# Second attention layer: turns, projections and merges in one piece behind a chunk's value product, in place of between the scores

## The chip, the cores and the metric

One core of one Trainium2 chip runs the whole kernel in one launch. The metric is the device time in microseconds (us); the number shown for a kernel is the median of its runs. The kernel is a raw program: each engine (TensorE, VectorE, ScalarE, GpSimd, SyncE for transfers) has its own list of instructions, written out in order by the Python code, and the engines meet only at semaphores. An instruction that waits holds up everything behind it on its engine.

## The reference

Two decoder layers on x of 4 batches x 512 tokens x 128 features. The part that the change touches is the attention of the second layer (`A1`), 16 heads of 8 features, without a mask:

```
q = proj(wq, bq); k = proj(wk, bk); v = proj(wv, bv)      # 4 x 16 heads x 512 x 8
scores = einsum('bhqd,bhkd->bhqk', q, k) / sqrt(8)
attn   = softmax(scores, axis=-1)
ctx    = einsum('bhqk,bhkd->bhqd', attn, v)
out    = einsum('bsd,ed->bse', ctx, wo) + bo
x      = x + out
```

Before it come a causal attention (`A0`), a cross attention on 77 context tokens (`X0`) and a mixture of experts (`M0`); behind it a second cross attention (`X1`, one head of 128) and a quantized convolutional feed-forward (`F1`). Every layer starts with a layer norm of x.

## The kernel before

**Units and chunks.** Attention works in units of one batch and four heads. Units 0 to 15 are `A0`, 16 to 31 `X0`, 32 to 47 `A1` (four units a batch). A unit of `A1` has four chunks c = 0 to 3, one for each 128 keys. In a chunk TensorE makes four scores i = 0 to 3, one for each head (`scores_pe`, L712: 128 keys x 512 queries), ScalarE takes the exponential of each (`exp_act`, L733), and TensorE multiplies the values with all four (`pv_pe`, L760, eight instructions in the trace). The value product of chunk c is issued one chunk late, behind the fourth score of chunk c+1; that of chunk 3 stands in chunk 0 of the next unit (`last_pv_pe`).

**Maxima.** The softmax's maximum is found one to two units ahead: 16 products a unit (`max_pe`, L597, one head, 128 queries x 512 keys), each reduced by VectorE (`max_dve`, L613). `maxima_beside` puts four of them in each chunk, one ahead of each score. Score and maximum product use 64 rows of the array each, the one the upper and the other the lower half, and run side by side: below, such a two is called a pair. When a unit's 16 maxima are there, GpSimd splits them (`neg_of`, L628 and L630), TensorE turns them (`turn_pe`, L635), VectorE copies them (`turn_dve`, L642) and a transfer puts them beside the queries (`shift_sp`, L649); the first score of that unit waits for it.

**Banks.** `A1`'s scores rotate over three PSUM banks (`SINGLES = 3`): score n waits until the exponential of score n-3 is done (L708). Maxima, turns, merges, projections and the like take turns in four further banks (`take_bank`). `out` in `take_bank` says for how many later takes a bank is passed over; with `OPEN` it is passed over until `close_bank`.

**What stands between.** TensorE also carries work on all 128 rows. `finish_pe` (L779, four transposes) turns the finished unit's output, and VectorE normalises it (`finish_dve`, L788 and L792). `BESIDE` gives each unit at most one further task at each of the places "a", "b" and "c": `norm_pe` (task "turn", L546), `stage_q_pe` (q and k, L863), `stage_v_pe` (L881), `merge_pe` (L802), `proj_pe` (L821), and those of the second cross attention (`cross_*`). q, k, v and proj come in two halves (part 0 and 1); all others are whole in part 0. ScalarE or VectorE then empties the bank.

In `A1` before the change `unit_pe` (L1048 to L1096) places them so, behind the score of the number given:

- c = 0: "a" part 0 behind score 0; behind score 3 the last value product of the unit before, then "a" part 1
- c = 1: behind score 3 the value product, then "b" part 0
- c = 2: `finish_pe` behind score 0; behind score 3 the value product, then `turn_pe`
- c = 3: "c" part 0 behind score 0; behind score 3 the value product, then "c" part 1

In `A1`'s sixteen units there are 15 finishes, 10 whole tasks at "c", 6 whole tasks at "a", 6 at "b", and 9 in halves (6 at "a", 3 at "c"). ScalarE does the copy that empties a whole task's bank between a chunk's second and third exponential (`in_one` is true for them, L1154), that of a task in halves behind the fourth (L1165, L1171).

Of the kernel before, what the change touches and what calls it, by code (L numbers as in the profile page):

```python
# [128 lines left out]
STREAMS = (range(0, 2 * UN), range(2 * UN, 3 * UN))  # L129


def layer(g):
    return ATTS[g // UN]
# [53 lines left out]
def finished_in(g):  # L187

    u = g - (2 if layer(g) is X0 else 1)
    if g == X0.first:  # L190
        return None
    return u if u >= 0 and last_of_stream(u) == last_of_stream(g) else None
# [30 lines left out]

def in_one(g, place):

    return layer(g) is not X0 and BESIDE.get((g, place), ("q",))[0] not in ("q", "k", "v")


MOMENTS_IN = {5: (X0, 0), 9: (X0, 1), 13: (X0, 2), 19: (X0, 3), 23: (M0, 0), 27: (M0, 1), 31: (M0, 2), 32: (A1, 2), 33: (A1, 3), 37: (X1, 0), 40: (F1, 0), 41: (X1, 1),
# [32 lines left out]
def build(nc, d, out):  # L262
# [4 lines left out]
    with es:  # L267
# [364 lines left out]
        def turn_pe(e, g):  # L632
            e.wait_ge(s["neg"], g + 1)
            bank = take_bank(e, ("turn", g))
            e.transpose(bank[:].bitcast(BF16)[0:8 * QT, 0:P], neg[:, g % 2].rearrange("p j c h q -> p (j c h q)"),  # L635
                        identb[:]).then_inc(is_filled(("turn", g)), 1)
# [128 lines left out]
        def last_pv_pe(e, g):  # L765
            pv_pe(e, g, layer(g).kt - 1)
# [278 lines left out]

        def unit_pe(e, g):  # L1048
            a, u = layer(g), finished_in(g)
            first = g == STREAMS[0].start or g == STREAMS[1].start  # L1050
            short[0] = a is X0
            for c in range(a.kt):
                beside = maxima_beside(g, c)
                for i in range(4):
                    for k in beside[i]:
                        max_pe(e, *k)
                    scores_pe(e, g, c, i)
                    if a is X0:
                        continue
                    if i == 0:  # L1060
                        if c == 0:
                            beside_pe(e, g, "a", 0)
                        if c == 1 and a is not A1:
                            for t in turned_in(g):
                                turn_pe(e, t)
                        if c == 2 and u is not None:
                            finish_pe(e, u)
                        if c == 3:
                            beside_pe(e, g, "c", 0)
                    if i == 3:  # L1070
                        if c:
                            pv_pe(e, g, c - 1)
                        elif not first:
                            last_pv_pe(e, g - 1)
                    if i == 3:
                        if c == 2 and a is A1:
                            for t in turned_in(g):
                                turn_pe(e, t)
                        if c == 0:
                            beside_pe(e, g, "a", 1)  # L1080
                        if c == 1:
                            beside_pe(e, g, "b", 0)
                        if c == 3:
                            beside_pe(e, g, "c", 1)
                            if g == X0.first - 1:
                                turn_pe(e, X0.first + 1)
            if a is X0:
                for part in range(2):
                    beside_pe(e, g, "a", part)
                last_pv_pe(e, g - 1)  # L1090
                if u is not None:
                    finish_pe(e, u)
                if g + 2 <= last_of_stream(g):
                    turn_pe(e, g + 2)
                for part in range(2):
                    beside_pe(e, g, "b", part)  # L1096

        def unit_dve(e, g):
            a, u = layer(g), finished_in(g)
            for c in range(a.kt):  # L1100
                beside = maxima_beside(g, c)
                for i in range(4):
                    for k in beside[i]:
                        max_dve(e, *k)
                    if a is A1 and c == 2 and i == 3:
                        for t in turned_in(g):
                            turn_dve(e, t)
                    if a is not X0 and i == 0:
                        if c == 1 and a is not A1:
                            for t in turned_in(g):  # L1110
                                turn_dve(e, t)
                        if c == 2 and u is not None:
                            finish_dve(e, u)
                if a is not X0 and c != 2:
                    beside_dve(e, g, "abbc"[c])
                if c == 2 and a is A0 and g in NORM_IN:
                    after, b = NORM_IN[g]
                    normalise(e, after.ln, b)
                if c == 3 and g == X0.first - 1:
                    neg_of(e, X0.first + 1)  # L1120
                    turn_dve(e, X0.first + 1)
                if c == 2 and g in INTEGERS_IN:
                    scales_dve(e, INTEGERS_IN[g])
# [21 lines left out]
        def turned_in(g):  # L1145

            return [g + 1] if g < last_of_stream(g) else []
# [1375 lines left out]
```

## Time and profile before

| | us |
|---|---|
| median of 3 runs (lowest, highest) | 780.21 (778.45, 782.99) |
| the profiled execution | 780.1 |
| its span | 778.2 |
| TensorE matmuls busy | 642.7 (83%) |
| TensorE weight loads busy | 351.0 (45%) |
| VectorE busy | 561.7 (72%) |
| ScalarE busy | 431.2 (55%) |
| GpSimd busy | 302.7 (39%) |

The shares are means over six very different layers. `A1` lies at about 488 to 699 us of the span. Matmuls overlap in the pipeline, so a busy TensorE is not one at its peak; the distance from one start to the next says more than an instruction's own duration.

### The profile page before, as it was taken

How to read it: one execution, taken by the hardware profiler on the slowest of the kernel's cores; microseconds unless marked ns; L12 is line 12 of the kernel's file. 1: busy time of each engine (PE TensorE's matmuls, PEld its weight loads, DVE VectorE, ACT ScalarE, POOL GpSimd, SP SyncE). 2: the span in 40 equal slices, each digit the busy share in tenths (PEclk: the TensorE clock that was granted, in tenths of full speed). 3: DMA queues.
4: the chain of work that ended last, by engine and by line, in shares of the span. 5: the costliest groups of instructions: out<-in, count | busy, mean ns of one | idle time of the engine just before them, and what ended most of it. 6: DMA issues, size and time to landing. Idle time of an engine off the chain costs nothing.

```text
span 778.2 us, 16034 instructions
## 1 busy us (share of the span) xinstructions
PE 642.7 (83%) x5015; PEld 351.0 (45%) x5020; DVE 561.7 (72%) x1672; ACT 431.2 (55%) x825; POOL 302.7 (39%) x536
## 2 busy tenths in 40 slices
PE   5679998989888884099997695879999989897987
PEld 2344454445344443089997581213332323234543
DVE  6877688786657876657778346997898998924564
ACT  1415565655756551055554540658878777783644
POOL 6653444555533157613335633144330331422210
PEclk9967999999999997589999985789999999998999
DMA  7744563462233221211121254000421010000000
GB/s 228 258 173 140 170 205 113 131 196 79 75 105 93 82 76 44 71 36 49 51 82 58 66 166 145 29 28 29 159 87 56 29 55 30 1 1 1 14 14 28
DMA packets 72802, 67.17 MB, mean 86 GB/s; under 512 B 14560, under 2 KB 67232, under 8 KB 72720
## 3 DMA queue, kind: packets, MB, share of 16 engines
q1 hardware_dynamic: 69920, 61.21, 25.5%
q0 software_dynamic: 2272, 4.69, 1.9%
q8 instruction: 42, 0.69, 0.4%
q14 instruction: 40, 0.33, 0.1%
q10 hardware_dynamic: 528, 0.26, 0.1%
HBM read 37.74 MB, written 28.00 MB: 84 GB/s over the span
## 4 chain that ended last, share of the span: by engine, by line
PE 52%; DVE 23%; issue 10%; POOL 7%; ACT 4%; DMA 2%; SPq 1%; DVEq 0%; ACTq 0%; POOLq 0%
DVE mx L613 12%; PE bank_pv L760 11%; PE bank_turn L597 7%; PE bank_scores L2156 6%; PE bank_scores L712 4%; PE bank_turn L1888 4%; PE bank_scores L1896 3%; PE bank_scores L1888 3%; POOL routed_tokens L1849 2%; PE bank_turn L779 2%; DVE stats L468 2%; ACT probs L733 2%; PE bank_turn L601 1%; DVE xn L489 1%; PE bank_turn L821 1%
## 5 line engine op out<-in xcount | busy, mean ns | idle before, releaser
L613 DVE TENSOR_REDUCE mx<-bank_turn 128x1 f32<-128x512 f32 (+4 forms) x439 | 251.2, 611 | 47.8 <-PE bank_turn L601 29.0
L597 PE MATMUL bank_turn<-stk 64*128 64x77 bf16 (+4 forms) x695 | 150.4, 302 | 33.8 <-DVE mx L613 21.7
L712 PE MATMUL bank_scores<-stk 64*128 64x512 bf16 (+3 forms) x576 | 171.2, 359 | 4.6 <-ACT probs L733 3.4
L737 ACT ACTIVATE probs<-bank_scores 128x1024 f32<-128x1024 f32 (+4 forms) x160 | 116.8, 768 | 91.3 <-PE bank_scores L712 90.2
L733 ACT ACTIVATE probs<-bank_scores 128x512 f32<-128x512 f32 x256 | 139.3, 605 | 40.6 <-PE bank_scores L712 39.7
L760 PE MATMUL bank_pv<-probs,vsl 128*32 128x512 f32 (+3 forms) x1152 | 138.9, 555 | 2.9 <-POOL probs L745 1.8
L597 PEld LDWEIGHTS bank_turn<-stk 64*128 64x128 bf16 x695 | 51.4, 96 | 130.2 <-DVE mx L613 62.7
L745 POOL TENSOR_SCALAR_AFFINE_SELECT probs<-probs 128x256 f32<-128x256 f32 x128 | 51.5, 407 | 72.0 <-ACT probs L737 70.4
L1865 POOL DMA_INDIRECT expert_outputs<-probs,y_at x39 | 38.0, 975 | 94.8 <-DVE y_at L1762 58.4
L712 PEld LDWEIGHTS bank_scores<-stk 64*128 64x128 bf16 x576 | 45.5, 94 | 28.2 <-ACT probs L733 16.0
L495 POOL TENSOR_TENSOR rstd<-var,mhalf 128x4 f32<-128x4 f32 x24 | 24.7, 1029 | 85.4 <-DVE var L474 85.2
L613 DVE TENSOR_REDUCE mx<-bank_scores 128x1 f32<-128x512 f32 x72 | 49.0, 681 | 8.7 <-PE bank_scores L597 8.2
L601 PE MATMUL bank_turn<-masked_key,later_key 64*128 64x64 bf16 x512 | 51.1, 200 | 0.0
L601 PEld LDWEIGHTS bank_turn<-masked_key,later_key 64*128 64x128 bf16 x512 | 45.8, 102 | 11.3 <-issue 2.9
L2156 PE MATMUL bank_scores<-f_w1c,w 128*128 128x512 f32 x96 | 48.3, 643 | 0.4 <-ACT w L555 0.4
L1896 PE MATMUL bank_scores<-w,oT 128*128 x312 | 43.6, 285 | 2.5 <-DVE probs L1782 2.5
L1888 PE MATMUL bank_turn<-probs,w_now 128*128 128x128 f32 x320 | 43.4, 285 | 0.8 <-DVE probs L1761 0.8
L1888 PEld LDWEIGHTS bank_turn<-probs,w_now 128*128 128x128 f32 x320 | 41.3, 202 | 1.1 <-DVE probs L1761 1.0
L1896 PEld LDWEIGHTS bank_scores<-w,oT 128*128 128x128 f32 x312 | 39.6, 199 | 3.7 <-issue 3.5
L597 PE MATMUL bank_scores<-stk 64*128 64x512 bf16 x72 | 30.3, 421 | 11.7 <-DVE mx L613 11.4
L1888 PE MATMUL bank_scores<-probs,w_now 128*128 128x128 f32 x304 | 39.3, 275 | 0.1
L628 POOL CAST neg<-mx 128x16 bf16<-128x16 f32 x33 | 6.5, 196 | 82.6 <-DVE mx L613 81.9
(323 smaller groups left out, 1078.7 us busy)
## 6 DMA issues: line engine op xcount, KB each, us to landing
stk<-stack_A SPq DMA_DIRECT2D x64, 256.0 KB, 3.1
w<-in_M_w SPq DMA_DIRECT2D x12, 512.0 KB, 4.6
stack_A<-parts SPq DMA_DIRECT2D x12, 384.0 KB, 2.7
stack_A<-fill SPq DMA_DIRECT2D x8, 512.0 KB, 4.9
stk<-stack_X SPq DMA_DIRECT2D x16, 256.0 KB, 2.6
stack_A<-parts SPq DMA_DIRECT2D x12, 256.0 KB, 3.1
probs<-routed_tokens SPq DMA_DIRECT2D x39, 65.0 KB, 1.8
stack_A<-parts SPq DMA_DIRECT2D x12, 128.0 KB, 3.0
```

What stands on the lines that cost most here:

```text
L597: mm = e.matmul(o, stk[r, slot, 0, pp, qt * P:(qt + 1) * P], stk[r, slot, 1, pp, 0:keys], start=True, stop=not a.causal)
L601: mm = e.matmul(o[:, qt * P + HR * k:qt * P + HR * (k + 1)], later_keys(j, k), masked_keys(j), start=False, stop=k == 1)
L613: e.tensor_reduce(o.rearrange("p h q -> p q h"), bank_of((g, m))[:, 0:k * keys].rearrange("p (q h k) -> p q h k", q=len(tiles), h=len(hs)) ...
L712: mm = e.matmul(score_bank(g, kt, i)[:, 0:S - q0], stk[r, slot, 1, pp, kt * P:(kt + 1) * P], stk[r, slot, 0, pp, q0:S], start=True, stop=True)
L733: e.activation(probs[:, probs_of(g, kt), j + 2 * pp], score_bank(g, kt, i), ACT.Exp, scale=1 / math.sqrt(HD)).then_inc(s["probs"], 1)
L737: e.activation(probs[0:a.kp, probs_of(g, kt), j:HG:2, 0:n], bank_scores[0:a.kp, 2 * j:2 * j + 2, 0:n], ACT.Exp, scale=1 / math.sqrt(HD)).t ...
L745: e.affine_select(out=o, in_=o, compare_op=ALU.is_ge, fill=0.0, base=0, pattern=[[0, 2], [1, P]], channel_multiplier=-1).then_inc(s["maske ...
L760: mm = e.matmul(bank_pv[VW * h:VW * (h + 1), q0:S], vsl[:, slot, kt, h, :], probs[:, probs_of(g, kt), h, 0:S - q0], start=(kt == 0), stop= ...
L1865: e.indirect_dma_start(scr_y, bass.IndirectOffsetOnAxis(ap=y_at[:, t:t + 1], axis=0), y_sb[:, t % 2], None).then_inc(m["stored"][t % 2], 16)
L1888: mm = e.matmul(hid[t % 2][z][:, c * P:(c + 1) * P], w_now[:, t % 2, o:o + P], x_inT[:, t % 2], start=True, stop=True)
L1896: mm = e.matmul(y_bank[:, 0:D], act[:, t % 2, c * P:(c + 1) * P], w2[:, bass.ds(ex[t], 1), c, :].rearrange("p o n -> p (o n)"), start=(c = ...
L2156: e.matmul(bank, f_xT[:, b, j * P + tap:j * P + tap + P], f_w1c[:, tap], start=(tap == 0), stop=False)
```

## The change

All of it is in `A1`. Every full-row task is taken out from between the scores; `full_rows_pe` issues them behind the fourth score, in this order: the value product, in chunk 1 the finish, in chunks 0, 1 and 3 both halves of "a", "b" or "c", in chunk 2 the turn. The finish moves from chunk 2 to chunk 1, on VectorE too, where it now stands behind all four maxima of chunk 1. `in_one` is true for `A0` alone, so ScalarE empties the banks of all of `A1`'s tasks behind the fourth exponential. `maxima_beside`, the scores, the value products, GpSimd's and SyncE's lists stay as they are.

```diff
-    return layer(g) is not X0 and BESIDE.get((g, place), ("q",))[0] not in ("q", "k", "v")
+    return layer(g) is A0 and BESIDE.get((g, place), ("q",))[0] not in ("q", "k", "v")
...
+        def full_rows_pe(e, g, c):
+
+            if c:
+                pv_pe(e, g, c - 1)
+            elif g != STREAMS[1].start:
+                last_pv_pe(e, g - 1)
+            if c == 1 and finished_in(g) is not None:
+                finish_pe(e, finished_in(g))
+            if c != 2:
+                for part in range(2):
+                    beside_pe(e, g, "ab.c"[c], part)
+            if c == 2:
+                for t in turned_in(g):
+                    turn_pe(e, t)
+
         def unit_pe(e, g):
...
                     scores_pe(e, g, c, i)
                     if a is X0:
                         continue
+                    if a is A1:
+                        if i == 3:
+                            full_rows_pe(e, g, c)
+                        continue
                     if i == 0:
                         if c == 0:
                             beside_pe(e, g, "a", 0)
-                        if c == 1 and a is not A1:
+                        if c == 1:
                             for t in turned_in(g):
                                 turn_pe(e, t)
...
                     if i == 3:
-                        if c == 2 and a is A1:
-                            for t in turned_in(g):
-                                turn_pe(e, t)
                         if c == 0:
                             beside_pe(e, g, "a", 1)
...
-                    if a is not X0 and i == 0:
-                        if c == 1 and a is not A1:
+                    if a is A0 and i == 0:
+                        if c == 1:
                             for t in turned_in(g):
                                 turn_dve(e, t)
                         if c == 2 and u is not None:
                             finish_dve(e, u)
+                if a is A1 and c == 1 and u is not None:
+                    finish_dve(e, u)
```

## Rows read from the trace of the kernel before

**Rows 1.** Busy time by stretch of `A1`: from:to, length, then each engine.
```profile
526.00:564.00 38.00, 35.67 (x241) 11.73 (x239) 30.97 (x57) 30.56 (x57) 15.98 (x27) 0.99 0.29 95
564.00:635.00 71.00, 64.20 (x448) 21.59 (x444) 66.14 (x152) 56.22 (x109) 20.64 (x39) 1.00 0.18 55
635.00:681.00 46.00, 42.27 (x290) 14.06 (x289) 41.65 (x95) 36.01 (x72) 14.47 (x28) 1.00 0.08 25
```
**Rows 2.** TensorE in order of time, unit 38's chunks 1 and 2: start, length, instruction, [idle].
```profile
576.68 0.39 PE L712 MATMUL bank_scores<-stk 64*128 64x512 bf16 x1
...
577.95 0.39 PE L712 MATMUL bank_scores<-stk 64*128 64x512 bf16 x1 [0.24 <-ACT probs L733]
578.27 1.06 PE L760 MATMUL bank_pv<-probs,vsl 128*32 128x512 f32 x8
...
579.27 0.39 PE L712 MATMUL bank_scores<-stk 64*128 64x512 bf16 x1
579.59 0.66 PE L779 MATMUL bank_turn<-ident,oT 128*128 128x128 f32 x4
...
580.93 0.64 PE L760 MATMUL bank_pv<-probs,vsl 128*32 128x512 f32 x4
```
**Rows 3.** TensorE, unit 41's chunk 3 and the start of unit 42.
```profile
620.49 0.39 PE L712 MATMUL bank_scores<-stk 64*128 64x512 bf16 x1
...
621.97 1.06 PE L760 MATMUL bank_pv<-probs,vsl 128*32 128x512 f32 x8
...
623.25 0.39 PE L712 MATMUL bank_scores<-stk 64*128 64x512 bf16 x1
```
**Rows 4.** TensorE, a unit of `X0`: value product, finish, turn and projection in one piece.
```profile
229.00 1.06 PE L760 MATMUL bank_pv<-probs,vsl 128*32 128x512 f32 x8
229.99 0.66 PE L779 MATMUL bank_turn<-ident,oT 128*128 128x128 f32 x4
230.58 0.23 PE L635 MATMUL bank_turn<-identb,neg 128*32 128x128 bf16 x1
230.74 1.16 PE L821 MATMUL bank_turn<-A_wo,okT 128*128 128x128 f32 x8
231.83 0.21 PE L597 MATMUL bank_turn<-stk 64*128 64x77 bf16 x1
```
**Rows 5.** TensorE, units 34 and 35: k and v in halves.
```profile
531.81 0.39 PE L712 MATMUL bank_scores<-stk 64*128 64x512 bf16 x1
532.12 0.70 PE L863 MATMUL bank_turn<-xnT,A_wk 128*128 128x256 f32 x2
532.76 0.60 PE L712 MATMUL bank_scores<-stk 64*128 64x512 bf16 x2
...
533.67 1.07 PE L760 MATMUL bank_pv<-probs,vsl 128*32 128x512 f32 x8
...
537.43 0.39 PE L597 MATMUL bank_turn<-stk 64*128 64x512 bf16 x1 [0.56 <-DVE mx L613]
```
**Rows 6.** TensorE, unit 39's chunk 1: first and fourth score.
```profile
587.96 0.39 PE L712 MATMUL bank_scores<-stk 64*128 64x512 bf16 x1
...
589.85 0.39 PE L712 MATMUL bank_scores<-stk 64*128 64x512 bf16 x1 [0.59 <-ACT probs L733]
```
**Rows 7.** ScalarE in order of time, units 38 to 40.
```profile
579.79 0.60 ACT L733 ACTIVATE probs<-bank_scores 128x512 f32<-128x512 f32 x1 [0.42 <-PE bank_scores L712]
...
583.82 0.58 ACT L560 COPY xnT<-bank_scores 128x512 f32<-128x512 f32 x1
...
605.01 1.14 ACT L2080 ACTIVATE w<-bank_scores,x_rec 128x128 f32<-128x128 f32 x4 [1.11 <-PE bank_scores L2071]
```
**Rows 8.** VectorE in order of time, unit 38 (maxima and finish).
```profile
580.37 0.25 DVE L788 RECIPROCAL rec<-bank_turn 128x16 f32<-128x16 f32 x1
580.65 0.29 DVE L792 TENSOR_TENSOR otok<-bank_turn,rec 128x128 f32<-128x128 f32 x1
...
582.78 3.16 DVE L613 TENSOR_REDUCE mx<-bank_turn 128x1 f32<-128x512 f32 x5
```

## The prediction

> **What bounds the kernel now.** I read the shares by stretch first. In `A1` three engines are close together [rows 1]: between 526 and 564 us TensorE is busy 35.7 of 38 us and VectorE 31.0; between 564 and 635 VectorE leads with 66.1 of 71 (TensorE 64.2); between 635 and 681 it is 42.3 and 41.7 of 46. ScalarE is never above 81%. The granted clock is 0.99 to 1.00, the upper of the two levels, so distances can be added as they stand. A share so high does not say what a microsecond more on TensorE costs; for that I read the order of time chunk by chunk, from one value product to the next.
>
> The reader should look at two neighbouring chunks [rows 2]. In chunk 1 of unit 38 nothing stands between the scores: first score at 576.68, fourth at 577.95 after an idle stretch put down to the exponential (L733), value product at 578.27, which is 1.59 us behind the first score. Another bare chunk needs 1.48 (620.49 to 621.97) [rows 3]. Three banks hold the scores, so the fourth waits for the first exponential: it begins 0.4 to 0.5 us behind the first score's start (0.52 from 579.27 [rows 2] to 579.79 [rows 7]) and takes 0.60 [rows 7]. The pairs follow one another at 0.22, so TensorE would reach the fourth score at 0.66 and comes to it at 1.16: in each bare chunk a hole of 0.5 us. In chunk 2 the finish stands in that hole: first score 579.27, finish 579.59, value product 580.93, which is 1.66 us [rows 2]. The finish takes 0.59 until the next work starts (229.99 to 230.58) [rows 4] and lengthens the chunk by only 1.66 - 1.48 = 0.18 (by 0.07 against the other bare chunk). That is the observation on which the forecast rests: what stands between the scores is nearly free now.
>
> **What each kind of step costs behind the value product.** The first cross attention already has such a piece [rows 4]: product to finish 0.99, finish to turn 0.59, turn to projection 0.16, both halves of the projection to the next pair 1.09. From a value product straight to a pair it is 1.00 (578.27 to 579.27, the first maximum starting with its score) [rows 2]. So the piece adds each task's full length: 0.59 for four transposes, 1.09 for a projection.
>
> Gains first. Each entry from pairs into a full-row task costs 0.32 from the pair's start (579.27 to 579.59) [rows 2] where pair to pair costs 0.22 (the second L712 of the two in 0.60 that start at 532.76, each 0.38 long) [rows 5]: 0.10 a time. Taken out are 15 + 10 + 6 + 9 = 40 entries: 4.0 us. Halves joined cost 1.09 instead of twice 0.64 (532.12 to 532.76, the halves of q, k, v and the projection alike) [rows 4, 5], so 0.19 x 9 = 1.7 us. Together 5.7 us of TensorE work.
>
> The Trainium skill, "TensorEngine Tiling (Array Packing)", Key Properties, says that changing the tiling mode drains the engine; that rule speaks for the change. The trace agrees, with 0.10 us for an entry. By this rule alone the time falls by the 5.7 us above; it is the first rival below, since it is silent on who waits meanwhile.
>
> Now the cost, by chunk. A bare chunk is 1.48 + 1.00 = 2.48.
>
> *Finishes (15).* Chunk 2 with the finish inside is 1.66 + 1.00 = 2.66; with the finish ahead of it in chunk 1's piece it is 0.59 + 2.48 = 3.07: +0.41. Six units run so (34, 36, 37, 38, 41, 45): +2.4. In 35 a norm turn at "b" already precedes: I take +0.3. In 40 and 44 the four activations L2080, 1.14 us [rows 7], hold back the first exponential whether the finish is inside or not, so the finish comes on top: +0.5 each, 1.0. In 46 and 47 there are no maxima left, and a finish inside lengthens nothing: +0.5 each, 1.0. In 39 and 43 the finish chunk is already as slow as a bare one plus 0.59, since VectorE first has the cross scores: 0. In 33 and 42 VectorE sets the pace: 0. Sum 4.7.
>
> *Whole tasks at "c" (10).* Chunk 3 drops by the 0.18 that four transposes inside cost, and by up to 0.3 more where the copy between its exponentials held up the fourth score. The next chunk 0 gets 0.59 more, and ScalarE's copy (0.58 [rows 7]), until now between the second and third exponential, stands ahead of that chunk's first: four transposes last 0.66 and the next work starts after 0.59 [rows 4], so the copy runs until some 0.7 behind the next pair's start, the first exponential begins then instead of at 0.5, and the fourth score slips by 0.2. Net 0.59 + 0.2 - 0.4, +0.4 each in 36, 38, 43, 46, 47; nothing in 32, 33, 40, 42, 44, where VectorE's moments or scales stand next to them. Sum 2.0.
>
> *Whole tasks at "a" (6).* Moving them out makes chunk 0 bare and puts 0.59 to 1.09 behind it. Before, their ScalarE copy stood among chunk 0's exponentials, so that those and the copy of the last value product ran into chunk 1, whose fourth score came 1.89 us behind its first (587.96 to 589.85) in place of 1.16 [rows 6]. Behind the longer piece ScalarE has caught up but for the one copy. What is added to chunk 0's piece comes back in chunk 1. I take -0.3 over all.
>
> *Halves (9).* The half inside costs 533.67 - 531.81 = 1.86 against 1.48, so 0.38 [rows 5]; it goes, and the half behind (0.64) becomes 1.09: +0.07 each, 0.6 in all. Against that stands a bank: it is taken at the first half and kept open over three maxima, and the fourth maximum then waits for VectorE, 0.56 idle at 537.43 [rows 5]. Joined, the bank is out only for the piece. TensorE sits so about 2 us in all, but ScalarE's copies ahead of the next chunk give half of it back. Net about 0.6 - 1.0 = -0.4.
>
> *What VectorE takes back.* Its maxima follow one another at 0.60 to 0.63 (five in 3.16), four make 2.4 a chunk; a finish adds 0.5 [rows 8]. In its busiest stretch, 564 to 635, 4.9 of 71 us are not busy [rows 1]. Where it is the bound, a longer piece on TensorE costs nothing while its four banks hold work, 2.4 us, and the longest piece is about 1.00 + 0.59 + 1.09 = 2.68. I have set six chunks to nothing above; the rest of such cover I put at 1 us. The turned maxima are no new bound: where chunk 3 is bare, the next unit's first score comes 1.28 behind the value product (621.97 to 623.25) instead of 1.00 [rows 3], because it waits for the transfer; that is so now and stays so, and a task at "c" covers it in either order.
>
> Sum: 4.7 + 2.0 - 0.3 - 0.4 - 1.0 = +5.0 us. The gain of 5.7 is inside these distances and not to be taken off again. The profiled execution took 780.1 (span 778.2, 1.9 around it), 0.1 from the median: 780.1 + 5.0 = 785.1. The bounds of the cost: if every finish and "c" task cost its full 0.59 and every copy 0.3, 25 x 0.59 + 10 x 0.3 = 17.8, less what the chunks drop now (25 x 0.18 = 4.5) and less the bank stalls of 2: +11, 791. From below: the whole gain, -5.7, and the bank stalls, -2: 772.
>
> **Rivals.** *The switches decide (faster).* If the hole before the fourth score does not open, because ScalarE still has a backlog after each piece or the maxima fill it, TensorE's own work counts and 40 entries and nine joins come off: -5.7, 774.4. It decides where TensorE is the only bound. For it: 35.7 of 38 us busy at 526 to 564 [rows 1]. Against: ScalarE has no backlog even now (0.42 idle until the score at 579.79) [rows 7]; a longer piece makes it idle more, not less.
>
> *VectorE hides it (no change).* If VectorE is the bound through 564 to 681 (107.8 of 117 us [rows 1]), only the terms outside count: units 34 to 36 (+1.3) and 46, 47 (+1.8), less freed bank stalls of 1 to 2: 781.5. Against: 9.2 us of that stretch VectorE is not busy, and a wait that the piece adds ahead of its finish is new idle time on the very engine that should be the bound.
>
> *Starved by the piece (slower still).* In chunk 1 VectorE's finish stands behind four maxima and waits for a finish that TensorE issues behind the value product, and in 39, 40, 43 and 44 for a further task. If VectorE then starts late and its lag spreads to the next chunk's banks, 0.3 us more in 15 units: +4.5 on top, 789.6.
>
> **How the numbers follow.** The forecast's mechanism gets 0.50, with 782 to 788 as its own range; the switches 0.20; VectorE 0.22; starved 0.08. What can be told from no change is 0.5%, 3.9 us: 776.3 to 784.1. Of the forecast's 0.50 a fifth lies below 784.1; starved is all slower: 0.48. Faster: most of the first rival, 0.18. The same: the remaining 0.34. The range, 775.5 to 789.5, leaves some 0.1 on each side.
>
> **What would show it.** Right: in the trace after, almost every chunk of `A1` has three pairs at 0.22, then 0.4 to 0.6 us without a start, then the fourth score; ScalarE's idle time before L733 grows by several us; chunk 2 of 37, 38, 41 takes 3.0 to 3.1 from value product to value product; waits of maxima for VectorE at L597 shrink. Everything outside `A1` keeps its length within 1 us. Wrong: fourth scores that follow at 0.22 behind the third, or chunks with a finish ahead that still take under 2.8. Then the switches count and the time falls. If VectorE is without idle time from 564 to 681, the second rival is right. If TensorE's granted clock falls below 1.00 in the new holes, none of the sums holds.

## The result, and the profile after

| | before | after |
|---|---|---|
| median us (runs) | 780.33 (16) | 784.68 (16) |
| lowest, highest | 778.45, 784.82 | 780.48, 787.34 |
| ratio, 95% interval | | 1.0046 (1.0027 to 1.0065) |
| span of the profiled execution | 778.2 | 785.1 |
| first score of unit 32 to the last value product of unit 47 ("the layer") | 210.55 | 215.32 |

The change costs about 3.6 us (0.0046 x 780; by the interval 2.1 to 5.1); the forecast was 5.0 and a time of 785.1. The layer itself grew by 4.77 us in the profiled execution. From the page after, its groups of maxima and exponentials (instructions | busy, mean ns | idle before, and what ended most of it):

```profile
L597 PE MATMUL bank_turn<-stk 64*128 64x77 bf16 (+4 forms) x699 | 149.7, 303 | 32.3 <-DVE mx L613 23.2
...
L733 ACT ACTIVATE probs<-bank_scores 128x512 f32<-128x512 f32 x256 | 133.3, 605 | 37.1 <-PE bank_scores L712 36.7
```

The stretches that answer to [rows 1] lie 4 to 5 us later, and the middle one is 1 us longer (from:to, length, then busy time of TensorE, its weight loads, VectorE, ScalarE and GpSimd, then the granted clock):

```profile
530.00:568.00 38.00, 35.25 (x230) 12.61 (x230) 29.74 (x55) 28.88 (x56) 16.31 (x27) 0.99 0.27 89
568.00:640.00 72.00, 66.09 (x450) 22.02 (x449) 65.58 (x148) 54.87 (x108) 19.82 (x36) 1.00 0.18 57
640.00:686.00 46.00, 41.42 (x283) 14.20 (x283) 41.49 (x96) 35.78 (x72) 12.97 (x27) 1.00 0.08 25
```

VectorE and ScalarE are busy for a smaller share than before in all three: in the middle one VectorE is idle 6.4 of 72 us, where 4.9 of 71 were idle. The granted clock is as it was. What was lost was lost to waits, and where they stand is read chunk by chunk. Unit 38's chunks 1 and 2, the place of [rows 2], on TensorE (start, length, instruction; the maxima of the pairs are left out):

```profile
584.09 1.06 PE L760 MATMUL bank_pv<-probs,vsl 128*32 128x512 f32 x8
585.09 0.66 PE L779 MATMUL bank_turn<-ident,oT 128*128 128x128 f32 x4
...
585.68 0.39 PE L712 MATMUL bank_scores<-stk 64*128 64x512 bf16 x1
...
585.90 0.59 PE L712 MATMUL bank_scores<-stk 64*128 64x512 bf16 x2
...
586.84 0.39 PE L712 MATMUL bank_scores<-stk 64*128 64x512 bf16 x1
587.16 1.07 PE L760 MATMUL bank_pv<-probs,vsl 128*32 128x512 f32 x8
```

The finish is in front now, the three pairs follow at once, and from the third to the fourth score the hole of the forecast is open again. From unit 34's chunk 2 on, 42 of 54 chunks look like this (two scores at 0.22 to 0.3 us and the fourth over 0.55 behind the third); before the change it was 6. From value product to value product this chunk takes 3.07 us, where 2.66 stood [rows 2]: the forecast's number for it.

Not all of it is in this pattern. At the start of unit 41 stands a wait that the forecast had expected to shrink:

```profile
617.33 0.66 PE L802 MATMUL bank_scores<-ident,otok 128*128 128x128 f32 x4
617.92 0.39 PE L597 MATMUL bank_turn<-stk 64*128 64x512 bf16 x1
...
619.82 0.39 PE L597 MATMUL bank_turn<-stk 64*128 64x512 bf16 x1 [1.08 <-DVE mx L613]
...
620.14 1.06 PE L760 MATMUL bank_pv<-probs,vsl 128*32 128x512 f32 x8
```

VectorE at the same time computes the moments of the next layer norm between two maxima:

```profile
617.68 0.29 DVE L468 BATCH_NORM_STATS2 stats<-x_sb 128x6 f32<-128x128 f32 x1
...
619.00 0.17 DVE L474 TENSOR_SCALAR var<-mv 128x4 f32<-128x4 f32 x1
619.08 2.48 DVE L613 TENSOR_REDUCE mx<-bank_turn 128x1 f32<-128x512 f32 x4
```

The fourth maximum needs a bank. The merge (L802) has taken one of the four, and that one is passed over for the next four takes (`out=4`), which are exactly this chunk's four maxima. So the fourth needs a bank that one of the first three has used, and VectorE, on its moments from 617.68, gives it back too late.

### The profile page after: what moved, and what is told of

It is laid out like the page before. It is cut to its first block, busy times and chain, and to the rows that moved or that the text cites. A ratio compares the mean times of both kernels' runs of the same rounds, so it can differ in the third digit from the quotient of the medians.

```text
span 785.1 us, 16034 instructions
## 1 busy us (share of the span) xinstructions
PE 648.6 (83%) x5015; PEld 354.1 (45%) x5020; DVE 562.6 (72%) x1672; ACT 428.6 (55%) x825; POOL 302.7 (39%) x536
## 4 chain that ended last, share of the span: by engine, by line
PE 53%; DVE 24%; issue 9%; POOL 7%; ACT 3%; DMA 2%; SPq 1%; DVEq 0%; ACTq 0%; POOLq 0%
DVE mx L613 14%; PE bank_pv L760 12%; PE bank_turn L597 6%; PE bank_scores L2174 5%; PE bank_scores L712 4%; PE bank_turn L1906 4%; PE bank_scores L1914 3%; PE bank_scores L1906 3%; PE bank_turn L779 3%; POOL routed_tokens L1867 2%; DVE stats L468 2%; PE bank_turn L601 1%; PE bank_scores L597 1%; DVE xn L489 1%; PE bank_turn L863 1%
## 5 line engine op out<-in xcount | busy, mean ns | idle before, releaser
L613 DVE TENSOR_REDUCE mx<-bank_turn 128x1 f32<-128x512 f32 (+4 forms) x443 | 253.3, 613 | 46.4 <-PE bank_turn L601 29.6
L597 PE MATMUL bank_turn<-stk 64*128 64x77 bf16 (+4 forms) x699 | 149.7, 303 | 32.3 <-DVE mx L613 23.2
L712 PE MATMUL bank_scores<-stk 64*128 64x512 bf16 (+3 forms) x576 | 168.5, 360 | 6.8 <-ACT probs L733 4.8
L733 ACT ACTIVATE probs<-bank_scores 128x512 f32<-128x512 f32 x256 | 133.3, 605 | 37.1 <-PE bank_scores L712 36.7
L760 PE MATMUL bank_pv<-probs,vsl 128*32 128x512 f32 (+3 forms) x1152 | 140.6, 561 | 2.8 <-POOL probs L745 1.8
L597 PEld LDWEIGHTS bank_turn<-stk 64*128 64x128 bf16 x699 | 51.6, 97 | 123.6 <-DVE mx L613 57.2
L613 DVE TENSOR_REDUCE mx<-bank_scores 128x1 f32<-128x512 f32 x68 | 46.3, 681 | 8.6 <-PE bank_scores L597 8.2
L2174 PE MATMUL bank_scores<-f_w1c,w 128*128 128x512 f32 x96 | 46.1, 618 | 0.4 <-ACT w L555 0.4
L597 PE MATMUL bank_scores<-stk 64*128 64x512 bf16 x68 | 28.5, 418 | 13.2 <-DVE mx L613 13.1
```

Source lines behind the costliest of these rows:

```text
L597: mm = e.matmul(o, stk[r, slot, 0, pp, qt * P:(qt + 1) * P], stk[r, slot, 1, pp, 0:keys], start=True, stop=not a.causal)
L613: e.tensor_reduce(o.rearrange("p h q -> p q h"), bank_of((g, m))[:, 0:k * keys].rearrange("p (q h k) -> p q h k", q=len(tiles), h=len(hs)) ...
L712: mm = e.matmul(score_bank(g, kt, i)[:, 0:S - q0], stk[r, slot, 1, pp, kt * P:(kt + 1) * P], stk[r, slot, 0, pp, q0:S], start=True, stop=True)
L733: e.activation(probs[:, probs_of(g, kt), j + 2 * pp], score_bank(g, kt, i), ACT.Exp, scale=1 / math.sqrt(HD)).then_inc(s["probs"], 1)
L760: mm = e.matmul(bank_pv[VW * h:VW * (h + 1), q0:S], vsl[:, slot, kt, h, :], probs[:, probs_of(g, kt), h, 0:S - q0], start=(kt == 0), stop= ...
L2174: e.matmul(bank, f_xT[:, b, j * P + tap:j * P + tap + P], f_w1c[:, tap], start=(tap == 0), stop=False)
```

## The experiments

For each kernel I take from its trace the layer's length and that of a quieter stretch, from unit 34's chunk 2 to the layer's end. From there on (in time: from the start of the value product in that chunk) equal chunks of different kernels agree to 0.01 us, and the granted clock is 1.00 in all of them. The part ahead of it contains transfers and less regular waits, and its granted clock differs from one profiled execution to the next, from 0.77 to 0.83 where whole tiles are worked on. So a layer's length contains some chance of the clock, and the stretch does not. Ratios are against the kernel before in the same group of runs, with their 95% interval; the median of the kernel before was 779.7 to 782.8 in these groups.

| kernel | layer | stretch | ratio |
|---|---|---|---|
| before | 210.55 | 167.83 | |
| changed | 215.32 | 171.36 | 1.0046 (1.0027 to 1.0065) |
| finish_behind | 213.88 | 169.89 | 1.0051 (1.0021 to 1.0081) |
| whole_behind | 212.17 | 169.26 | 1.0008 (0.9980 to 1.0035) |
| halves_joined | 207.98 | 166.73 | 0.9997 (0.9972 to 1.0023) |
| behind_third | 207.55 | 166.34 | 0.9981 (0.9952 to 1.0009) |
| banks_back | 212.06 | 169.78 | 0.9983 (0.9950 to 1.0015) |
| third_joined | 206.23 | 165.52 | 0.9914 (0.9881 to 0.9947) |
| third_joined_back | 204.64 | 164.75 | 0.9932 (0.9904 to 0.9960) |
| copies_later | 215.21 | 169.34 | 1.0047 (1.0019 to 1.0074) |
| joined_later | 215.37 | 173.20 | 1.0070 (1.0037 to 1.0102) |
| short_between | 182.45 | 148.39 | 0.9639 (0.9597 to 0.9680) |
| short_behind | 188.69 | 150.81 | 0.9656 (0.9611 to 0.9701) |

A layer's length is of one profiled execution; the ratio is of all runs and decides on the whole. Its intervals are 1.5 to 3.5 us to each side.

### The finishes alone

```diff
-                        if c == 2 and u is not None:
+                        if c == 2 and a is A0 and u is not None:
                             finish_pe(e, u)
...                                       # i == 3, behind pv_pe
+                        if c == 1 and a is A1 and u is not None:
+                            finish_pe(e, u)
```

(VectorE's finish moves with it, as in the change.)

> The kernel before with the 15 finishes alone moved behind the value product of chunk 1, on TensorE and VectorE as the change has it. All other tasks stay between the scores. Theory (the hole before the fourth score is left empty): A1, from the first score of unit 32 to the last value product, grows from 210.6 us by the 4.7 of the forecast's finish term; chunk 2 goes from 2.66 to 3.07 us where no maximum waits. Rival (the switches decide): 15 entries at 0.10 go away, A1 shrinks by 1.5. Rival (VectorE hides it): under +1.5.

The layer grows by 3.33 us, the stretch by 2.06, and the kernel is slower, 1.0051. In the order of time (unit 37's chunk 2) the finish again stands ahead, and the fourth score comes late:

```profile
569.28 1.06 PE L760 MATMUL bank_pv<-probs,vsl 128*32 128x512 f32 x8
570.28 0.66 PE L779 MATMUL bank_scores<-ident,oT 128*128 128x128 f32 x4
...
572.04 0.39 PE L712 MATMUL bank_scores<-stk 64*128 64x512 bf16 x1
572.35 1.06 PE L760 MATMUL bank_pv<-probs,vsl 128*32 128x512 f32 x8
```

3.07 again. This part alone accounts for most of the loss, 2.1 of 3.5 us in the stretch. Of the 1.3 us ahead of it, 0.7 are not the finishes' at all. Unit 32's chunk 2 has the same instructions in both kernels, before and then here:

```profile
495.42 1.45 PE L760 MATMUL bank_pv<-probs,vsl 128*32 128x512 f32 x8
...
498.28 1.07 PE L760 MATMUL bank_pv<-probs,vsl 128*32 128x512 f32 x8
```

```profile
497.37 1.93 PE L760 MATMUL bank_pv<-probs,vsl 128*32 128x512 f32 x8
...
500.94 1.07 PE L760 MATMUL bank_pv<-probs,vsl 128*32 128x512 f32 x8
```

It takes 2.86 us at a granted clock of 0.86 in the one and 3.57 at 0.58 in the other.

### The whole tasks alone

```diff
+        def joined(g, place):
+            task = BESIDE.get((g, place), (None,))[0]
+            return layer(g) is A1 and task not in ("q", "k", "v", "proj")
...
-                        if c == 0:
+                        if c == 0 and not joined(g, "a"):
...                                       # "c" likewise; at i == 3, behind the product:
+                            if joined(g, "a"):
+                                beside_pe(e, g, "a", 0)
```

(`in_one` is true in `A0` alone, as in the change.)

> The kernel before with only the whole tasks at a and c (turns, merges, the cross attention's) moved behind the value product, and ScalarE's copies behind the fourth exponential. Finishes and the halves stay. Theory: +2.0 for the tasks at c and -0.3 for those at a, A1 +1.7 us. Switches decide: 16 entries, -1.6. VectorE hides it: within 0.7 of nothing.

The layer grows by 1.62 us, 1.43 of them in the stretch; over all runs 1.0008, which cannot be told from no change. The forecast's 1.7 is met, but not term by term. A task at "a" of 39, 43 and 47 makes chunk 1 longer by 0.51, 0.51 and 0.33, and this does not come back. Against that, chunk 3 of 42 alone falls by 1.46 (3.98 to 2.52), of which the next chunk takes 0.73.

### The halves alone

The same edit with `task in ("q", "k", "v", "proj")` and `in_one` as before.

> The kernel before with only the nine tasks in halves (q, k, v, projection) joined behind the value product. Theory: A1 -0.4 us (the bank is out for a shorter time, one half is no longer covered). Switches decide: nine entries and nine joins, -2.6. If the bank kept open over three maxima is what costs most: -2 or more as well, but then the waits of the maxima for VectorE in these chunks are gone, where the switches alone would leave them.

The layer shrinks by 2.57 us, where -0.4 was forecast; the whole time cannot be told from no change (0.9997). Where the forecast had looked, in 35 and 36, it was right: chunk 0 falls by 0.36 and chunk 1 grows by 0.44. The gain lies elsewhere. Unit 34's chunks 0 and 1 are together 1.2 shorter, and at the starts of units 41 and 45 the kernel before has the projection's first half between the scores and keeps its bank open, so that the fourth maximum waits for VectorE's moments:

```profile
610.71 0.39 PE L712 MATMUL bank_scores<-stk 64*128 64x512 bf16 x1
611.03 0.71 PE L821 MATMUL bank_turn<-A_wo,okT 128*128 128x128 f32 x4
...
613.33 0.39 PE L597 MATMUL bank_scores<-stk 64*128 64x512 bf16 x1 [1.05 <-DVE mx L613]
```

With the halves joined the chunk has all four banks:

```profile
607.39 1.06 PE L760 MATMUL bank_pv<-probs,vsl 128*32 128x512 f32 x8
608.39 0.39 PE L712 MATMUL bank_scores<-stk 64*128 64x512 bf16 x1
...
609.31 0.39 PE L597 MATMUL bank_turn<-stk 64*128 64x512 bf16 x1
609.79 0.39 PE L712 MATMUL bank_scores<-stk 64*128 64x512 bf16 x1
610.11 1.06 PE L760 MATMUL bank_pv<-probs,vsl 128*32 128x512 f32 x8
```

It takes 2.72 in place of 3.94 us (unit 45's 2.61 for 3.84). Two thirds of that come back within the unit: the whole projection stands ahead of chunk 1 (+0.48), and in chunk 2 VectorE is late instead (+0.33). What is left is 0.4 a unit.

### Into the hole, in place of out of it

If the hole before the fourth score is what makes an inserted task cheap, the best place is right ahead of that score, behind the third.

```diff
-                    if i == 0:
+                    if i == (2 if a is A1 else 0):
```

(On TensorE; the same on VectorE for the finish.)

> The kernel before with the inserted tasks behind the third score in place of behind the first, so right in the hole before the fourth; nothing is joined. Theory: the fourth score comes no later than now, and the second and third exponential and maximum come 0.6 us earlier, so ScalarE and VectorE wait less: A1 -2 us, between -5 and 0. If the place between the scores does not matter, only being among them: 0. If a task that sits in the hole delays the fourth score (task issued at 0.66, its end at 1.35, as now): also 0, with the same chunk of 2.66 us around a finish.

The layer shrinks by 3.00 us; over all runs 0.9981, whose interval holds 1. The chunk with the finish did not get shorter (2.73 against 2.67); half of the gain lies ahead of the stretch, and in the stretch, 1.5 us shorter, the largest gains are in chunk 1 of units 39 and 43, 2.79 in place of 3.20, and of 47, 2.80 in place of 3.38, and at the start of 41 and 45, 0.3 each. In 39's chunk 0, where the task stands, the second score now starts 0.23 behind the first in place of 1.38, and so its exponential comes earlier; in chunk 1 the first exponential then starts 0.78 behind its score in place of 1.19. The hole was well filled before; what it gains is that ScalarE is fed sooner.

### The parts together, and the banks

The three parts add up to 3.33 + 1.62 - 2.57 = +2.4, the change to +4.8. Set side by side chunk by chunk, the other 2.4 us stand in a few places: +1.0 at the start of unit 41 and +0.9 at that of 45 (less 0.3 in each one's chunk 2), +0.8 in unit 34 and +1.0 in 33's chunk 2, less 0.5 in 32's chunk 2, where the part with the finishes had the lower clock. In the stretch alone the parts add up to 2.06 + 1.43 - 1.10 = +2.4, the change to +3.5, so that 1.1 are left over. At 41 and 45 that is the gain of the joined halves, gone again: where the projection's bank had been open, the merge's is now passed over. The next kernel tests this. It is the changed one, in which `A1`'s tasks let their bank be taken again after three takes:

```diff
+            if soon_back[0] and out != OPEN:
+                out = min(out, 3)
```

(and the same in `close_bank`; `soon_back[0]` is true in `A1`)

> The changed kernel with the banks of A1's full-row tasks given back to the maxima after three later takes in place of four to ten. A1 took 210.6 us before, 215.3 changed; finishes alone behind the product gave +3.3, whole tasks alone +1.6, halves alone -2.6, together +2.4 where the change has +4.8. Theory: the 2.4 that the parts don't explain are banks: each piece now ends right ahead of the four maxima of the next chunk, its bank is passed over for exactly these, so the fourth maximum waits for VectorE with three banks (0.35, and 0.7 to 1.1 where moments stand next). Given back after three, the fourth maximum takes the task's bank, which ScalarE has emptied by then, and A1 comes to 213 us, the waits of the fourth maximum gone. Rival: the waits are VectorE's load, A1 stays at 215.3 within 0.4.

```profile
615.15 0.38 PE L601 MATMUL bank_turn<-stk 64*128 64x512 bf16 x1
615.56 0.39 PE L601 MATMUL bank_scores<-stk 64*128 64x512 bf16 x1
616.04 0.39 PE L716 MATMUL bank_scores<-stk 64*128 64x512 bf16 x1
```

This is the place of the 1.08 us shown above (lines are 4 further down). The fourth maximum takes the merge's own bank, which ScalarE has emptied by then, and no longer waits for the moments: from value product to value product 3.23 in place of 3.80. The layer is 3.26 us shorter than the changed kernel's, and the kernel as a whole stands at 0.9983, not to be told from the kernel before. The places are few: unit 34 (1.9; its longest wait was 3.67 us in the changed kernel and is 1.90 here; 3.37 in the kernel before) and chunk 0 of 41, 43, 38 and 45 (0.57, 0.38, 0.32, 0.30; these are the 1.6 by which the stretch is shorter). So the banks are shown at these places; 33's chunk 2 stays as long as in the changed kernel, and its 1.0 us is not explained. The rest of the 1.0 and 0.9 at 41 and 45 is the length of the merge itself, ahead of a chunk that was bare with the halves alone.

One thing does not move: a chunk behind a norm, with its `[0.35 <-DVE mx L613]` ahead of the fourth maximum, keeps its 3.15 us although the wait is gone. There the exponential of the first score ends last, and the 0.35 lay inside that wait.

### Both gains in one kernel

The halves joined and all other inserts behind the third score, on the kernel before.

> The kernel before with the two halves joined behind the value product, and the finishes and whole tasks still between the scores but behind the third. Alone these gave A1 -2.6 and -3.0 us. If they act at different chunks, A1 is 205.0 us (-5.6) and the time some 0.6% under before; if both only take the same idle time of VectorE, -3.5.

```profile
611.65 0.66 PE L802 MATMUL bank_scores<-ident,otok 128*128 128x128 f32 x4
612.24 0.39 PE L712 MATMUL bank_scores<-stk 64*128 64x512 bf16 x1
612.55 1.07 PE L760 MATMUL bank_pv<-probs,vsl 128*32 128x512 f32 x8
...
615.04 1.06 PE L760 MATMUL bank_pv<-probs,vsl 128*32 128x512 f32 x8
616.03 1.16 PE L821 MATMUL bank_turn<-A_wo,okT 128*128 128x128 f32 x8
```

The merge fills the hole ahead of the fourth score, chunk 0 behind it is bare (2.49), and the projection stands in one piece behind it. This kernel is clearly faster than before: median 776.61 in seven runs, 0.9914 of the kernel before (0.9881 to 0.9947), with a layer 4.3 us shorter, between the two expected values. The ratio makes it 6.7 us; the runs of the kernel before beside it had a median of 782.83, and the difference to the layer is not explained. (In unit 41 the finish waits 0.3 us for VectorE, and its chunk takes 3.01 where 2.67 stood before; with the halves alone it was 2.99.)

> The kernel with halves joined behind the product and the rest behind the third score (A1 206.2), now with the banks given back to the maxima after three takes, as in banks_back, where this took 3.3 us from the changed kernel. Theory: the gain was where VectorE's moments meet three banks; with joined halves two such places are left (38, 34), so A1 205.5, within 0.7. If giving banks back helps as much here: 203.

The same with banks back after three takes: 204.64 us for the layer, 775.67 and 0.9932 (0.9904 to 0.9960). The layer is 1.6 us shorter than third_joined's and 0.2 under the lower end of what was expected; in the stretch it is 0.8, most of it in 38's chunk 0 (4.23 to 3.65), one of the two places that I had named. Unit 34, the other, did not gain. The two versions cannot be told apart by their times.

### The hole itself

If the forecast's hole is the reason for the finish's price, that price must fall when the hole is small. In these two kernels `A1`'s exponentials and maxima take only the first 128 of 512 columns; the orders are the kernel before's (between) and the changed one's (behind). The edit of the exponentials; that of the maxima, in `max_dve`, takes the same 128 columns:

```diff
-                    e.activation(probs[:, probs_of(g, kt), j + 2 * pp], score_bank(g, kt, i), ACT.Exp,
+                    e.activation(probs[:, probs_of(g, kt), j + 2 * pp, 0:P], score_bank(g, kt, i)[:, 0:P], ACT.Exp,
```

> The kernel before, but in A1 each exponential and each maximum takes only the first 128 of 512 columns, so that ScalarE and VectorE have far less to do and the instructions, waits and TensorE's work stay the same. To be read against short_behind alone. With 0.25 to 0.3 us in place of 0.60 the first exponential is done 0.8 us behind the first score, so the hole before the fourth is 0.15 in place of 0.5.

> The changed kernel with the same cut: first 128 of 512 columns in A1's exponentials and maxima. If the change costs time because ScalarE's first exponential leaves a hole that is no longer filled, the sign turns here: TensorE's own work decides, 40 entries and nine joins, up to 5.7 us less, of which holes of 0.15 in 40 places without an insert take back some: A1 shorter than in short_between by 0 to 5. If the change costs time for a reason on TensorE itself, A1 stays longer by 4 to 5.

```profile
555.57 1.07 PE L765 MATMUL bank_pv<-probs,vsl 128*32 128x512 f32 x8
556.56 0.66 PE L784 MATMUL bank_turn<-ident,oT 128*128 128x128 f32 x4
557.15 0.39 PE L717 MATMUL bank_scores<-stk 64*128 64x512 bf16 x1
...
558.00 0.39 PE L717 MATMUL bank_scores<-stk 64*128 64x512 bf16 x1
558.32 1.06 PE L765 MATMUL bank_pv<-probs,vsl 128*32 128x512 f32 x8
```

The fourth score comes 0.85 behind the first in place of 1.16, so the hole is 0.2 in place of 0.5. A chunk with the finish ahead takes 2.75; with the finish inside, in the other order (columns as above):

```profile
551.02 1.06 PE L765 MATMUL bank_pv<-probs,vsl 128*32 128x512 f32 x8
552.34 0.66 PE L784 MATMUL bank_turn<-ident,oT 128*128 128x128 f32 x4
553.68 1.07 PE L765 MATMUL bank_pv<-probs,vsl 128*32 128x512 f32 x8
```

2.66. The finish's price is 0.09 where it was 0.40. So for the finish the hole is shown. The sum did not follow: I had expected the two kernels to be level or the order "behind" to be up to 5 us faster, and its layer is 6.24 us longer, more even than the 4 to 5 that I had put down for a reason on TensorE itself. Of that 3.8 lie ahead of the stretch, where I have no account of them (the granted clock there is 0.89 in the one and 0.81 in the other), and 2.4 in it. Among these are the whole tasks, whose copy of 512 columns ScalarE still has ahead of the next chunk's first exponential (chunk 1 of 39, 43 and 47 takes 3.39 in place of 2.27), and the two chunks with finish and cross output, 4.27 in place of 3.88. My expectation had carried the finish's small price over to everything. So the empty hole is shown as the price of a finish, and not as that of the whole change. Over all runs the two are at 0.9639 and 0.9656, with intervals that overlap.

### ScalarE's copy out of the way

That copy is the second part of what a moved task costs. Here the changed kernel issues it on ScalarE behind the next chunk's second exponential (`exp_act` with j = 0 issues the first two):

```diff
+                if a is A1 and c < 3:
+                    of, place = ((g - 1, "c"), (g, "a"), (g, "b"))[c]
+                    if of >= A1.first and (place == "b" or not in_one(of, place)):
+                        beside_act(e, of, place)
```

> The changed kernel with ScalarE's copies of A1's tasks moved from behind the fourth exponential to behind the second one of the next chunk, so that they no longer stand ahead of the next chunk's first exponential. TensorE, VectorE, GpSimd and the transfers as in the changed kernel. Theory: in a chunk behind a piece the fourth score starts 1.24 (norm turn) to 1.34 us (q, k, merge, cross q) behind the first score and 1.78 behind the cross output, against 1.16 in a bare chunk, because the copy delays the first exponential. Moved, all come to about 1.16: some 8 x 0.08 + 11 x 0.17 + 2 x 0.6 = 3.7, less where VectorE paces: A1 from 215.3 to 212.5 (211.5 to 213.5). Rival: the fourth score waits for the fourth maximum's bank (0.35 idle for VectorE is booked there), and that is what sets it; then A1 stays at 215.3, or grows since the bank comes back later.

Chunk by chunk it did what was expected: with q and k 3.55 in place of 3.71, norm 3.07 for 3.15, merge 3.08 for 3.24, cross queries 3.55 for 3.70, finish and cross output 4.04 for 4.59. The stretch is 2.0 us shorter: these give 2.7, and chunk 3 of 40 and 44 loses 0.7. But the layer was to come to 212.5 and is 215.21: ahead of the stretch 1.9 us are lost again, in unit 32's chunks 1 (8.50 in place of 7.35) and 2 (3.56 in place of 2.79). The second of these ran at a granted clock of 0.68 against 0.88, so this loss is in part the clock's; the first I cannot account for. The whole time did not move, 1.0047.

> third_joined_back, with the copies of the joined halves and of the tasks at b behind the second exponential of the next chunk. Theory as in copies_later: 5 q and k by 0.17, 2 v by 0.1, 2 cross outputs by 0.5: A1 2 us less than third_joined_back. Rival: nothing, or longer, since q and k reach GpSimd's split and the transfers later.

The same on the best order with early banks turned out badly: 10.7 us more in the layer than third_joined_back, where 2 less were expected. I had put down "longer" as a rival, but for another reason (q and k reaching GpSimd later). With a bank back after three takes the fourth maximum takes the very bank that waits for the delayed copy (L897 is the copy of q and k):

```profile
555.72 0.39 PE L601 MATMUL bank_scores<-stk 64*128 64x512 bf16 x1 [1.41 <-ACT cos_sin L897]
556.03 1.07 PE L764 MATMUL bank_pv<-probs,vsl 128*32 128x512 f32 x8
...
560.33 0.39 PE L601 MATMUL bank_turn<-stk 64*128 64x512 bf16 x1 [1.42 <-ACT cos_sin L897]
560.65 1.07 PE L764 MATMUL bank_pv<-probs,vsl 128*32 128x512 f32 x8
```

That is 4.62 us a chunk where 3.71 stood. In units 40 and 44 the finish, right behind the third score, waits for the cross output's delayed copy (1.96 us in 40), and chunk 2 takes 5.75 in place of 4.36. My theory had counted ScalarE's order and not the bank behind it. `out=4` and `out=3` are a price in one neighbourhood and a guard in the other.

## Why the prediction was right, and where it was not

**The sign and the mechanism.** Work moved out of the hole costs its length, the hole stays. For the finishes this is shown by the chunks (2.67 to 3.07 in 34, 37, 38, 41 and 45), by the finishes alone (1.0051) and by the smaller price in a smaller hole.

**The finishes, forecast 4.7.** Measured +3.3 in the layer, of which 0.7 are the lower clock in unit 32; in the stretch +2.1, where the forecast had 4.3. So this term was too high by about half, although the price of a single finish was met. By chunk: +0.40 where 0.41 was forecast; 0.40 for 0.5 in 40 and 44; 0.58 and 0.40 for 0.5 in 46 and 47. Too high were 36 and 35 (0.14 and 0.22 for 0.41 and 0.3). And left out were gains: units 39 and 43 fell from 4.11 to 3.92, and chunk 3 behind the moved finish fell by 0.2 to 0.3 in 36, 37 and 38, and chunk 0 of 42 and 46 by 0.26 and 0.27.

**The whole tasks, 2.0 and -0.3.** Measured +1.62, so the sum was right, but by luck. What chunk 0's piece gained at "a" was to come back in chunk 1; chunk 1 grew instead, by 1.5 us in 39, 40, 43, 44 and 47 together. At "c", chunk 3 and the next chunk 0 were to add up to +0.4 in each of five units. They give +0.64 in 36, -0.36 in 38, 0.0 in 43, +0.24 in 46 and 47 each, and -0.73 in 42, which the forecast had set to nothing. (Behind 38, 42, 43 and 46 that chunk 0 also loses its own task at "a", so the two terms cannot be told apart fully.)

**The halves, -0.4.** Measured -2.57 (-1.1 in the stretch). Its pattern for k and v [rows 5] held. What it lacked were unit 34 (1.2), whose longest wait for VectorE falls from 3.37 to 2.45 us with the halves joined, and units 41 and 45 (0.4 each net).

**VectorE's cover, -1.0.** None is seen. The change costs 2.4 us more than its parts alone (1.1 in the stretch). At 41 and 45 whole tasks now stand right ahead of four maxima and their banks are passed over for exactly these four: where VectorE has the moments next to them, its lateness is paid in full. Giving the banks back takes 3.3 us away (1.6 in the stretch); in 33's chunk 2 it gives nothing back, so the banks are not the whole of the rest. So the total was met, 5.0 against 4.8 in the layer, with luck: this term and those of the finishes and halves have opposite signs: (3.3 - 4.7) + (1.6 - 1.7) + (-2.6 + 0.4) + (2.4 + 1.0) = -0.3. A right total is not a proof of its terms.

**Signs named ahead.** The three quick pairs and the late fourth score are there. ScalarE's idle time before L733 did not grow by several us: 37.1 after, and 40.6 before. Over the whole layer its idle time did grow, from 49.9 to 57.6 us; but part of it now stands ahead of the copies:

```profile
618.03 0.69 ACT L810 ACTIVATE okT<-bank_scores,A_bv 128x512 f32<-128x512 f32 x1 [0.59 <-PE bank_scores L802]
618.61 2.27 ACT L733 ACTIVATE probs<-bank_scores 128x512 f32<-128x512 f32 x4
```

TensorE's waits for VectorE at L597 were to shrink and grew, in the layer from 13.9 to 17.9 us (both forms).

**Outside the layer.** It was to keep its length within 1 us. Ahead of it the profiled executions differ by 4.1 us (488.05 and 492.18), behind it by 2.0 the other way, with the same instructions. The rows between 200 and 300 us, before and then after, show a lower granted clock after (0.98, 0.95):

```profile
200.00:300.00 100.00, 80.84 (x781) 40.78 (x778) 69.07 (x313) 58.98 (x81) 41.25 (x80) 0.98 0.27 79
```

```profile
200.00:300.00 100.00, 83.93 (x788) 41.05 (x788) 67.67 (x289) 60.09 (x83) 39.97 (x80) 0.95 0.28 81
```

So the 7 us between the two spans are 4.8 of the change and the rest not of it; the ratio of the runs, 3.6 us (2.1 to 5.1), agrees with that.

**The rivals.** *The switches decide*: refuted, the time rose. The rows do show the 0.10 an entry and 0.19 a join, so the rule of the Trainium skill, "TensorEngine Tiling (Array Packing)", Key Properties, that a change of mode drains the engine, is not contradicted; the saved drain only makes a hole longer. Of the 5.7 us that the forecast put down to that rule, 4.0 are entries; the 1.7 of the joins do not follow from it. *VectorE hides it*: refuted for the sum, VectorE is idle more; it would have given +1.4. *Starved by the piece*: its wait is there and small. VectorE waits 0.33 to 0.44 us for such a finish, 2.7 us in seven of them, and the chunks of such finishes take the 3.07 of the forecast and no more:

```profile
585.78 0.26 DVE L788 RECIPROCAL rec<-bank_turn 128x16 f32<-128x16 f32 x1 [0.37 <-PE bank_turn L779]
```

**What stays open.** The first units of the layer. From the first score to unit 34's chunk 2 the kernels with whole tiles take 39.9 to 45.9 us, and I can follow only the banks' part of it in unit 34 and the clock's in unit 32; the stretch behind carries the argument. The 1.0 us in 33's chunk 2 is open, and so is most of what the two kernels with a quarter of the columns differ by. Nor is it shown why the two best versions cannot be told apart although their layers differ by 1.6 us.

## What to carry to other kernels

Before moving work out from between two waiting instructions, measure the distance without it: if the hole stays when the work goes, the work was nearly free there, whatever switching it costs. Give each moved task its whole train: the copy that empties its bank, who stands behind that copy, and for how many takes the bank is missing and which takes those are. And test the parts one by one even if the total comes out as forecast.

## What was not expected of the hardware

A quarter of the columns does not make the hole a quarter. One exponential takes 0.28 us in place of 0.60 (128 and 512 columns), but the first one still begins 0.52 behind its score's start (557.15 above), as with the whole tile [rows 2, 7]:

```profile
557.67 1.03 ACT L738 ACTIVATE probs<-bank_scores 128x128 f32<-128x128 f32 x4 [1.69 <-PE bank_scores L717]
```

So the fourth score comes 0.85 behind the first in place of 1.16: the fixed delay sets the hole as much as the work does.

The same instructions ahead of the layer took 484.0 to 492.8 us in thirteen profiled executions, more than the whole effect under study, while equal chunks inside it, at a granted clock of 1.00, agree to 0.01 us. They fall into two groups by the granted clock from 200 to 300 us: in the five executions where it was 0.95 they took 490.0 to 492.8, in the eight where it was 0.98 they took 484.0 to 489.4. What sets the one or the other is not known from these runs. For a change of 0.5% in one layer the distances inside it are the sharper measure, and the ratio over many runs the check on them.
